# Latent stage: the last 64 latent columns on both halves of the partitions, and two short products of a round on row tiles side by side

## The chip, the cores and the metric

The kernel runs on one core of one Trainium2 chip. What is compared is the device time of one execution, in microseconds (us). The core has TensorE (PE; its weight loads are shown as PEld), VectorE (DVE), ScalarE (ACT), GpSimd (POOL) and SyncE (SP), each with a queue of its own. Matmul results go to PSUM, which has eight banks of 128 partitions x 512 f32 numbers.

## The reference, cut to what matters

The whole is a decoder of twelve blocks on a (16, 128, 256) input; each block is followed by a residual addition and a layer norm. The block of this change is latent attention (`_L2_attn_ref`), on 16 sequences of 128 tokens:

```python
c_q = _rmsnorm(x @ w_q_down.T, q_norm_w)            # 192 latent columns
q = (c_q @ w_q_up.T).reshape(b, t, H, NOPE + ROPE)  # 16 heads, 128 + 64
q_nope, q_rope = (q[..., :NOPE], q[..., NOPE:])
kv = x @ w_kv_down.T                                # 64 latent + 64 rotary
q_rope = _apply_rope(q_rope, cos, sin)
kv_up = (_rmsnorm(c_kv, kv_norm_w) @ w_kv_up.T).reshape(b, t, H, NOPE + VD)
scores = einsum(q_full, k_full) * scale             # causal, softmax
out = einsum(attn, v).reshape(b, t, H * VD) @ w_o.T
```

The kernel doesn't expand keys and values: the part of the key's up-projection is multiplied into the query's weights once (step "a"), that of the values into the output weights (step "b"), and the heads work on the 64 latent columns of the keys directly. A query of a head is then 64 rotary and 64 latent columns, both made from the 192 latent columns of `c_q`.

## The kernel before

The stage is the class `Latent` (line 1951 on). `order()` (L1997) writes the order of the work out by hand, and every engine walks it in the same order with its own method: `tensor` (L2020), `scalar` (L2119), `vector` (L2184), `gpsimd` (L2262). Engines meet through semaphores; `room[b]` is the event after which bank `b` may be written again, and each engine's queue is strictly in order.

The tokens are taken in four groups `g` of 512 (four sequences), and in each group eight pairs of heads: 32 units `u`. A round `t` of the loop runs several steps for units at different depths: "sw" and "q" (e = 0 and 1, the two heads of the pair) for u = t, "s" (scores) for u = t - 1, "t" (transposes of the probabilities) and "o" for u = t - 2, "acc" for u = t - 3. The order within a round is sw, t(0), s(0), q(0), t(1), s(1), q(1), o, acc. In rounds with t modulo 8 from 2 to 7 of the first three groups, one shared step for the next group stands ahead of "sw": dn, tr0, tr1, tr2, r0, r1.

- Step "dn" makes the latent columns of a group, "tr0" and "tr1" turn the first 128 and the last 64 of them (L2060), and ScalarE keeps them as `CQ[gs]` with 512 tokens in a row: `CQ[:, 0, :]` holds latent columns 0 to 127, `CQ[0:64, 1, :]` columns 128 to 191 (L2161).
- Step "sw" (L2078) makes the rotary part with its pairs exchanged, for both heads at once, in bank 2: two products, over 128 and over 64 rows. VectorE multiplies it by the sines into `M2` (L2223).
- Steps "q" (L2078 too) make rotary and latent part of one head in bank 3, again over 128 and over 64 rows. ScalarE copies the latent half to `QA` (L2171), VectorE multiplies the rotary half by the cosines (L2230) and adds `M2` (L2232). With L2232 bank 3 is free again: `room[3]`.
- Step "s" fills bank 4 with the causal mask (L2084) and four products (L2087). VectorE takes the maximum (L2236) and scales it (L2237), ScalarE the exponentials (L2177), VectorE the reciprocal (L2241), and GpSimd multiplies (L2268). `room[4]` comes with the exponentials.
- Step "t" is L2095 with VectorE's copy L2246, "o" L2102, "acc" L2113 in banks 0 and 1.

An f32 product shows as two matmul instructions ("passes") in the profile, each with a weight load of its own; a transpose shows as one. The weights are loaded by `load` (L1965) on SP's queue, in two sets with a semaphore each, while the stage before still runs.

## Time and profile before

| | |
|---|---|
| time, median of 3 runs | 4290.99 us (4288.17 to 4293.5) |
| the profiled execution's own time | 4302.71 us |
| its span, first to last instruction | 4300.9 us |
| its mean granted TensorE clock | 0.924 of full speed |
| busy: PE, DVE, ACT, POOL | 3705.8, 3159.7, 1976.4, 968.1 us |
| costliest lines of this stage on the page | L2078 (lCQ, lq) 142.6 us; L2177 90.6 us; L2268 66.6 us |

A share of busy time is a mean over twelve different stages. The groups of lines count a matmul from its start to the end of its flow through the array, so that back to back matmuls overlap by some tenths of a microsecond; how fast they follow each other is read from the starts. "Idle before" is time in which the engine had nothing running ahead of that group, and the name behind it what ended the wait.

### The profile page before, as it was taken

Reading aid. Unit: us, or ns where it says so; the run is one execution under the profiler, and the core shown is the slowest. Engines: PE = TensorE matmul, PEld = TensorE weight load, DVE = VectorE, ACT = ScalarE, POOL = GpSimd, SP = SyncE. Lnnn points to the kernel's source line nnn. Section 1 sums busy time; section 2 is a strip of 40 time slices with the busy share of each in tenths; the row PEclk is TensorE's granted clock in tenths of the full one; section 3 lists DMA queues with packets and bytes.
Section 4 is the critical chain, followed back from the end, with each engine's and each line's share of the span. In section 5 each row is a group of like instructions: output and inputs, shape, how many; then the busy total and the mean of one; then the engine's idle time right before and its main releaser. Section 6 shows DMA issues by size and latency. Waiting matters only on the chain.

```text
span 4300.9 us, 69538 instructions
## 1 busy us (share of the span) xinstructions
PE 3705.8 (86%) x25052; PEld 2244.1 (52%) x25068; DVE 3159.7 (73%) x7102; ACT 1976.4 (46%) x4701; POOL 968.1 (23%) x1237
## 2 busy tenths in 40 slices
PE   7799999998851858798999989869999999997985
PEld 3466666665531436644555555645555555554543
DVE  7788989887567665533566568758888888886678
ACT  4466666665521324212333334336556555563345
POOL 2433321344111000000111122023323233233220
PEclk9999999999975988898999989989999999997887
DMA  2222222222110100020000000300000000001000
GB/s 68 69 63 70 62 60 59 63 67 49 35 62 0 33 22 2 1 72 21 1 1 1 1 30 2 122 0 1 1 1 1 1 1 1 1 1 47 1 1 20
DMA packets 220707, 120.09 MB, mean 28 GB/s; under 512 B 115280, under 2 KB 213200, under 8 KB 219152
## 3 DMA queue, kind: packets, MB, share of 16 engines
q1 hardware_dynamic: 220368, 115.65, 9.6%
q8 instruction: 203, 3.33, 0.3%
q14 instruction: 136, 1.11, 0.1%
HBM read 100.89 MB, written 14.68 MB: 27 GB/s over the span
## 4 chain that ended last, share of the span: by engine, by line
PE 61%; DVE 24%; issue 5%; ACT 5%; POOL 3%; SPq 1%; DMA 1%; DVEq 0%; ACTq 0%; POOLq 0%
PE ps L305 20%; PE ps L3111 5%; PE ps L2078 3%; PE ps L2803 3%; PE ps L3099 3%; PE ps L2816 2%; PE ps L2782 2%; PE ps L497 2%; PE ps L2113 1%; POOL dTB L826 1%; PE ps L2596 1%; PE ps L575 1%; DVE macc L3243 1%; POOL dtmp L825 1%; DVE hMX L2871 1%
## 5 line engine op out<-in xcount | busy, mean ns | idle before, releaser
L305 PE MATMUL ps<-xT,min 128*128 128x512 f32 (+1 forms) x1072 | 536.8, 629 | 7.1 <-DVE mZ L3238 4.8
L3243 DVE SCALAR_TENSOR_TENSOR macc<-ps,mcw,macc 128x508 f32<-128x508 f32 (+2 forms) x408 | 302.9, 742 | 149.0 <-ACT macc L3167 139.4
L3181 ACT ACTIVATE mE<-ps,mcol 128x128 f32<-128x128 f32 x1024 | 291.3, 370 | 8.4 <-PE ps L3081 1.5
L305 PEld LDWEIGHTS ps<-xT,min 128*128 128x128 f32 (+1 forms) x1072 | 183.3, 191 | 191.2 <-issue 182.0
L3329 POOL TENSOR_TENSOR mE<-mE,mCB 128x512 f32<-128x512 f32 x128 | 163.7, 1279 | 482.3 <-ACT mE L3181 482.3
L3111 PE MATMUL ps<-mwo,macc 128*128 128x256 f32 x1024 | 246.1, 383 | 19.2 <-DVE macc L3277 19.2
L2841 ACT ACTIVATE hE<-ps 128x512 f32<-128x512 f32 x256 | 139.0, 594 | 223.4 <-PE ps L2803 223.4
L3336 POOL TENSOR_TENSOR mSQ<-mSQ,mtn 128x512 f32<-128x512 f32 x128 | 163.5, 1277 | 259.5 <-ACT mtn L3185 259.5
L2177 ACT ACTIVATE lP<-ps,lm 128x128 f32<-128x128 f32 x256 | 90.6, 366 | 266.1 <-DVE lm L2237 266.1
L3111 PEld LDWEIGHTS ps<-mwo,macc 128*128 128x128 f32 x1024 | 186.1, 191 | 47.3 <-DVE macc L3277 25.7
L2871 DVE TENSOR_REDUCE hMX<-ps 128x2 f32<-128x512 f32 x256 | 158.9, 684 | 57.9 <-PE ps L2782 57.9
L2268 POOL TENSOR_TENSOR lP<-lP,lm 128x512 f32<-128x512 f32 x64 | 66.6, 1041 | 574.5 <-DVE lm L2241 574.5
L821 POOL TENSOR_TENSOR dTB<-did,dNB 128x1024 f32<-128x1024 f32 (+1 forms) x10 | 28.7, 2871 | 664.4 <-DMA dNB<-d_N 599.0
L727 DVE SCALAR_TENSOR_TENSOR dav<-ps,dsmall,dav 128x508 f32<-128x508 f32 (+2 forms) x192 | 142.4, 742 | 47.2 <-ACT dav L598 42.5
L826 POOL TENSOR_TENSOR dTB<-dTB,dtmp 128x30 f32<-128x30 f32 (+11 forms) x300 | 170.3, 568 | 23.5
L727 DVE SCALAR_TENSOR_TENSOR daq<-ps,dsmall,daq 128x508 f32<-128x508 f32 (+2 forms) x192 | 142.5, 742 | 44.3 <-ACT daq L598 38.9
L2803 PE MATMUL ps<-hXE,hKE 32*128 32x256 f32 x1024 | 163.2, 440 | 13.4 <-DVE hXE L2877 7.9
L825 POOL TENSOR_TENSOR dtmp<-dNB,dTB 128x30 f32<-128x30 f32 (+11 forms) x300 | 155.4, 518 | 23.5
L497 PE MATMUL ps<-dKQ 128*128 128x256 f32 x512 | 137.7, 396 | 26.7 <-ACT dO L673 17.3
L727 DVE SCALAR_TENSOR_TENSOR dak<-ps,dsmall,dak 128x508 f32<-128x508 f32 (+2 forms) x192 | 142.3, 741 | 24.1 <-ACT dak L598 19.5
L3167 ACT ACTIVATE macc<-ps,ms,mcw 128x512 f32<-128x512 f32 x136 | 105.9, 779 | 116.6 <-PE ps L305 116.6
L2078 PE MATMUL ps<-lCQ,lq 128*128 128x512 f32 (+1 forms) x256 | 142.6, 656 | 17.7 <-DVE lQA L2232 17.7
(593 smaller groups left out, 8931.7 us busy)
## 6 DMA issues: line engine op xcount, KB each, us to landing
dwk<-in_L_attn_Wk SPq DMA_DIRECT2D x64, 128.0 KB, 2.3
dwq<-in_L_attn_Wq SPq DMA_DIRECT2D x64, 128.0 KB, 2.4
dwv<-in_L_attn_Wv SPq DMA_DIRECT2D x64, 128.0 KB, 2.4
dwg<-in_L_attn_Wg SPq DMA_DIRECT2D x64, 128.0 KB, 2.4
dwo<-in_L_attn_Wo SPq DMA_DIRECT2D x64, 128.0 KB, 2.6
min<-in_m_in SPq DMA_DIRECT2D x2, 4096.0 KB, 17.7
d_N<-dNT SPq DMA_DIRECT2D x256, 16.0 KB, 1.5
dTT<-d_TT SPq DMA_DIRECT2D x256, 16.0 KB, 1.9
```

The lines of the kernel that those rows point to most:

```text
L305: t = pe.matmul(out, w[:, j, :], self.c.xT[:, j, blk(g, 512)], start=j == 0, stop=j == 1)
L497: t = pe.matmul(bank(4 + i)[:, blk(j, 256)], self.KQ[s][:, 2 * i + j, 0, :], self.KQ[s][:, 2 * i + j, :, :], start=True, stop=True)
L727: x = dve.scalar_tensor_tensor(out=acc[:, :, 3 - j:T], in0=p[:, :, 0:T - 3 + j], scalar=small[:, 4 * k + j:4 * k + j + 1], in1=acc[:, :, 3 ...
L825: then(pool.tensor_tensor(part, bc(NB[:, s, s + 1:32], s, True), bc(TB[:, s, 0:s], 31 - s), ALU.mult))
L826: then(pool.tensor_tensor(low, low, part, ALU.subtract))
L2078: t = pe.matmul(bank(b), w, self.CQ[gs][0:K, i, :], start=i == 0, stop=i == 1)
L2803: t = pe.matmul(bank(4 + i)[:, blk(lt, 256)], self.KE[x][r, e, blk(lt)], self.XE[x][r, e, :], start=True, stop=True)
L2871: m = dve.tensor_reduce(self.MX[y][:, k, 32 * r:32 * r + 32:16], bank(r).rearrange("p (e n) -> p e n", e=2), AX.X, ALU.max, negate=True)
L3111: t = pe.matmul(bank(j // 2)[:, blk(j % 2, 256)], self.acc[s][:, blk(j)], self.wo[:, i, :], start=i == 0 and j % 2 == 0, stop=i == 31 and ...
L3181: x = act.activation(self.E[s][:, e, blk(j)], bank(4 + e)[:, blk(j)], ACT.Exp, bias=self.col[:, 4 * g + j, 0, 2 * i + e:2 * i + e + 1])
L3243: x = dve.scalar_tensor_tensor(out=acc[:, :, 3 - j:T], in0=p[:, :, 0:T - 3 + j], scalar=self.cw[:, i, j:j + 1], in1=acc[:, :, 3 - j:T], op ...
L3329: pool.tensor_tensor(g4(self.E[s][:, 0, :]), g4(self.E[s][:, 0, :]), self.CB[g % 2][:, :, :], ALU.mult).then_inc(*self.m0.up)
```

## The change

The last 64 latent columns are kept on both halves of the partitions (`CQ[:, 1, :]`, 128 partitions). To get them there, "tr1" adds to each of its four transposes a product with the identity into partitions 64 to 127 of bank 6, and ScalarE's copy takes all 128 partitions, with a scale laid out likewise (`n2`). The query weights of these 64 rows lie on both halves too for the rotary part (one more load of 512 KB; two small ones for `n2`); for the latent part, made in step "a", heads alternate: the even head of a pair lies on partitions 64 to 127, the odd one on 0 to 63. In "a" the outputs of the second kind go to the two column halves in turn, and ScalarE copies them with two instructions instead of one.

In the rounds, the product of q(e=0) over 64 rows moves ahead into "sw": between the product over 128 rows into bank 2 and that over rows 0 to 63 into bank 2 stands the one over rows 64 to 127 into bank 3. It opens the sum in bank 3, and q(e=0) closes it with its product over 128 rows, without a wait on bank 3. Instead "sw" waits for `room[3]`. Step q(e=1) stays as it was.

```diff
@@ -1961,15 +1962,16 @@
         self.q, self.sw_ = c.f32("lq", 2, 16, 128), c.f32("lsw", 2, 1024)
         self.qT, self.kvT = c.f32("lqT", 16, 192), c.f32("lkvT", 16, 2, 64)
         self.wo, self.cs = c.f32("lwo", 16, D), c.f32("lcs", 2, T)
+        self.n2 = c.f32("ln2", 3)
 
     def load(self, sp):
         i = self.ins
         self.may_load(sp)
         self.fetch(sp, 0, (self.dn[:, :, :], i["l_dn"].rearrange("(c p) n -> p c n", p=128)), (self.nw[:, :], i["l_nw"]),
-                   (self.cs[:, :, :], i["c_rope"]))
+                   (self.n2[64:128, :], i["l_nw"][0:64, :]), (self.n2[0:64, :], i["l_nw"][0:64, :]), (self.cs[:, :, :], i["c_rope"]))
         q = self.q[:, :, :, :].rearrange("p c h n -> p c (h n)")
         self.fetch(sp, 1, (self.qT[:, :, :], i["l_qT"]), (self.kvT[:, :, :, :], i["l_kvT"]),
-                   (q[:, 0, :], i["l_q"][0:128, :]), (q[0:64, 1, :], i["l_q"][128:192, :]),
+                   (q[:, 0, :], i["l_q"][0:128, :]), (q[0:64, 1, :], i["l_q"][128:192, :]), (q[64:128, 1, :], i["l_q"][128:192, :]),
                    (self.sw_[:, 0, :], i["l_sw"][0:128, :]), (self.sw_[0:64, 1, :], i["l_sw"][128:192, :]),
                    (self.wo[:, :, :], i["l_wo"].rearrange("(h p) n -> p h n", p=128)))
 
@@ -2019,7 +2021,7 @@
 
     def tensor(self, pe):
         c, bank, room = self.c, self.c.bank, self.c.room
-        pe.wait_ge(self.dma[1], 112)
+        pe.wait_ge(self.dma[1], 128)
         for step, g, u, e in self.order():
             s, gs, pr = u % 4, g % 2, u % 8
             if step == "a":
@@ -2027,8 +2029,8 @@
                 rows = 64 if i else 128
                 pe.wait_ge(*room[g])
                 for h in range(8):
-                    t = pe.matmul(bank(g)[0:rows, blk(h, 64)], self.qT[:, 8 * n + h, 128 * i:128 * i + rows], self.kvT[:, 8 * n + h, 0, :],
-                                  start=True, stop=True)
+                    to = bank(g)[blk(1 - h % 2, 64), blk(h, 64)] if i else bank(g)[:, blk(h, 64)]
+                    t = pe.matmul(to, self.qT[:, 8 * n + h, 128 * i:128 * i + rows], self.kvT[:, 8 * n + h, 0, :], start=True, stop=True)
                 t.then_inc(*self.am.up)
                 room[g] = self.ac.at(g + 1)
             elif step == "b":
@@ -2044,7 +2046,7 @@
             elif step == "dn":
                 pe.wait_ge(*c.xt_ready(self.n, g))
                 if g == 0:
-                    pe.wait_ge(self.dma[0], 48)
+                    pe.wait_ge(self.dma[0], 80)
                 for h in range(2):
                     pe.wait_ge(*room[6 + h])
                     for j in range(2):
@@ -2058,6 +2060,8 @@
                 pe.wait_ge(*self.cn.at(g + 1))
                 for j in range(4):
                     t = pe.transpose(bank(6)[0:n, blk(j)], self.CN[gs][:, j, lo:lo + n], c.ident[:, :])
+                    if n == 64:
+                        t = pe.matmul(bank(6)[64:128, blk(j)], self.CN[gs][:, j, lo:lo + n], c.ident[:, :], start=True, stop=True)
                 t.then_inc(*self.trn.up)
                 room[6] = self.kept.at(3 * g + i + 1)
             elif step in ("r0", "r1"):
@@ -2067,15 +2071,24 @@
                 room[7] = self.rot.at(2 * g + n + 1)
             elif step in ("sw", "q"):
                 n, b = (0, 2) if step == "sw" else (e + 1, 3)
-                pe.wait_ge(*room[b])
+                if (n, e) != (1, 0):
+                    pe.wait_ge(*room[b])
                 if n == 0:
                     pe.wait_ge(*self.kept.at(3 * g + 3))
                     pe.wait_ge(*self.kr.at(g + 1))
                 if u == 0:
                     pe.wait_ge(*self.ac.at(4))
-                for i, K in enumerate((128, 64)):
-                    w = self.sw_[0:K, i, blk(pr)] if n == 0 else self.q[0:K, i, 2 * pr + e, :]
-                    t = pe.matmul(bank(b), w, self.CQ[gs][0:K, i, :], start=i == 0, stop=i == 1)
+                CQ = self.CQ[gs]
+                if n == 0:
+                    pe.wait_ge(*room[3])
+                    pe.matmul(bank(2), self.sw_[:, 0, blk(pr)], CQ[:, 0, :], start=True, stop=False, skip_group_check=True)
+                    pe.matmul(bank(3), self.q[64:128, 1, 2 * pr, :], CQ[64:128, 1, :], start=True, stop=False, skip_group_check=True)
+                    t = pe.matmul(bank(2), self.sw_[0:64, 1, blk(pr)], CQ[0:64, 1, :], start=False, stop=True, skip_group_check=True)
+                elif e == 0:
+                    t = pe.matmul(bank(3), self.q[:, 0, 2 * pr, :], CQ[:, 0, :], start=False, stop=True, skip_group_check=True)
+                else:
+                    pe.matmul(bank(3), self.q[:, 0, 2 * pr + 1, :], CQ[:, 0, :], start=True, stop=False)
+                    t = pe.matmul(bank(3), self.q[0:64, 1, 2 * pr + 1, :], CQ[0:64, 1, :], start=False, stop=True)
                 t.then_inc(*self.up.up)
                 room[b] = self.m2.at(u + 1) if n == 0 else self.qa.at(2 * u + e + 1)
             elif step == "s":
@@ -2119,8 +2132,8 @@
     def scalar(self, act, own):
         c, bank = self.c, self.c.bank
         self.before(act)
-        act.wait_ge(self.dma[0], 48)
-        act.wait_ge(self.dma[1], 112)
+        act.wait_ge(self.dma[0], 80)
+        act.wait_ge(self.dma[1], 128)
         for step, g, u, e in self.order():
             s, gs = u % 4, g % 2
             if step == "last":
@@ -2128,10 +2141,15 @@
                 continue
             if step == "a":
                 n, i = divmod(g, 2)
-                rows = 64 if i else 128
                 act.wait_ge(*self.am.at(g + 1))
-                act.copy(self.q[0:rows, i, 8 * n:8 * n + 8, :].rearrange("p (q e) n -> p q (e n)", e=2)[:, :, 64:192],
-                         bank(g)[0:rows, :].rearrange("p (q n) -> p q n", n=128)).then_inc(*self.ac.up)
+                if i == 0:
+                    x = act.copy(self.q[:, 0, blk(n, 8), :].rearrange("p (q e) n -> p q (e n)", e=2)[:, :, 64:192],
+                                 bank(g).rearrange("p (q n) -> p q n", n=128))
+                else:
+                    for e in range(2):
+                        half = blk(1 - e, 64)
+                        x = act.copy(self.q[half, 1, 8 * n + e:8 * n + 8:2, half], bank(g)[half, :].rearrange("p (q e n) -> p q e n", e=2, n=64)[:, :, e, :])
+                x.then_inc(*self.ac.up)
             elif step == "b":
                 act.wait_ge(*self.bm.at(g + 1))
                 act.activation(self.B[:, blk(g, 2), :], bank(2 + g).rearrange("p (q n) -> p q n", q=2), ACT.Copy,
@@ -2151,14 +2169,13 @@
                 o.then_inc(*self.sqs.up)
             elif step in ("tr0", "tr1", "tr2"):
                 i = int(step[2])
-                n = self.TURNS[i][1]
                 act.wait_ge(*self.trn.at(3 * g + i + 1))
                 if g >= 2 and i == 0:
                     act.wait_ge(*self.up.at(24 * g - 24))
                 if g >= 2 and i == 2:
                     act.wait_ge(*self.sc.at(16 * g - 16))
                 if i < 2:
-                    x = act.activation(self.CQ[gs][0:n, i, :], bank(6)[0:n, :], ACT.Copy, scale=self.nw[0:n, i:i + 1])
+                    x = act.activation(self.CQ[gs][:, i, :], bank(6), ACT.Copy, scale=self.n2[:, 1:2] if i else self.nw[:, 0:1])
                 else:
                     act.activation(self.KK[gs][64:128, 0, :], bank(6)[64:128, :], ACT.Copy, scale=self.nw[64:128, 2:3])
                     x = act.activation(self.KK[gs][0:64, 1, :], bank(6)[0:64, :], ACT.Copy, scale=self.nw[0:64, 2:3])
@@ -2184,7 +2201,7 @@
     def vector(self, dve, own):
         c, bank = self.c, self.c.bank
         dve.wait_ge(*self.c.xn.at(4 * self.n))
-        dve.wait_ge(self.dma[0], 48)
+        dve.wait_ge(self.dma[0], 80)
 
         def then(ins):
```

## Rows read from the trace of the kernel before

**Rows 1.** TensorE in a stretch of the stage: length, busy us (and instructions) per engine, granted clock.
```profile
2060.00:2160.00 100.00, 93.22 (x456) 53.61 (x455) 54.50 (x117) 34.39 (x145) 13.54 (x13) 1.00 0.00 1
```

**Rows 2.** Chain of waits of one round: start us, us, what ran.
```profile
2406.32 0.07 DVE lm L2241
2406.43 0.69 DVE lQA L2230
2407.15 1.02 DVE lQA L2232
2408.22 2.18 PE ps L2078 x4
```

**Rows 3.** The stage's waits (2000 to 2490): us in total, times, longest.
```profile
PE ps L2078 <- DVE lQA L2232: 17.7, 29, 1.5
PEld ps L2084 <- ACT lP L2177: 15.9, 32, 2.3
```

**Rows 4.** TensorE's timeline of the same round: start us, us, count at the end.
```profile
2400.05 2.07 PE L2078 MATMUL ps<-lCQ,lsw 128*128 128x512 f32 x4
2403.65 2.08 PE L2078 MATMUL ps<-lCQ,lq 128*128 128x512 f32 x4
2405.66 0.66 PE L2095 MATMUL ps<-ident,lP 128*128 128x128 f32 x4
2406.35 0.39 PE L2084 MATMUL ps<-identb,neg 128*128 128x512 bf16 x1
2410.32 1.09 PE L2102 MATMUL ps<-lPT,lCN 128*64 128x128 f32 x16
```

**Rows 5.** Timeline: four passes without a change of tiling.
```profile
2330.95 1.88 PE L305 MATMUL ps<-xT,ldn 128*128 128x512 f32 x4
```

**Rows 6.** Timeline: passes on four, and on two row tiles, in other stages.
```profile
1514.34 2.00 PE L1289 MATMUL ps<-rQE,rKT 32*128 32x512 f32 x16
2533.38 1.13 PE L2803 MATMUL ps<-hXE,hKE 32*128 32x256 f32 x8
```

**Rows 7.** Timeline: the end of that round and the next "sw".
```profile
2412.08 0.91 DVE L2232 TENSOR_TENSOR lQA<-lQA,lM 64x512 f32<-64x512 f32 x1
2412.97 0.41 PEld L2078 LDWEIGHTS ps<-lCQ,lsw 128*128 128x128 f32 x2
2413.18 0.59 PE L2078 MATMUL ps<-lCQ,lsw 128*128 128x512 f32 x1
```

**Rows 8.** Timeline: four transposes in a round, and tr1 in the prologue.
```profile
2198.69 0.60 PE L2060 MATMUL ps<-ident,lCN 128*128 128x128 f32 x4
2199.13 0.59 PE L2078 MATMUL ps<-lCQ,lsw 128*128 128x512 f32 x1
1993.75 1.06 PE L2060 MATMUL ps<-ident,lCN 128*64 128x128 f32 x4 [0.78 <-ACT lCQ L2161]
```

**Rows 9.** Timeline: rounds 0 and 1.
```profile
2014.90 4.08 PE L2078 MATMUL ps<-lCQ,lsw 128*128 128x512 f32 x4
2015.73 0.69 DVE L2232 TENSOR_TENSOR lQA<-lQA,lM 64x512 f32<-64x512 f32 x1
2021.02 3.34 PE L2078 MATMUL ps<-lCQ,lq 128*128 128x512 f32 x4
```

**Rows 10.** Timeline: ScalarE after the copies of step "a".
```profile
1983.11 0.33 ACT L2147 ACTIVATE lCN<-ps 128x192 f32<-128x192 f32 x1 [1.34 <-PE ps L311]
```

**Rows 11.** The clock: stretches with it at half or kept, and one q(e=1).
```profile
2160.17:2170.41 10.24, 9.21 (x32) 5.60 (x33) 4.76 (x9) 4.23 (x17) 2.08 (x2) 0.50 0.00 0
2470.78:2474.20 3.42, 3.42 (x22) 2.77 (x22) 1.03 (x3) 1.71 (x9) 0.44 (x1) 0.50 0.02 5
1508.00:1521.00 13.00, 6.01 (x72) 2.98 (x64) 12.28 (x40) 6.67 (x17) 0.00 (x0) 1.00 0.00 0
1547.00:1560.00 13.00, 7.07 (x77) 3.99 (x70) 10.52 (x35) 3.27 (x9) 0.00 (x0) 0.76 0.00 0
2163.31 3.92 PE L2078 MATMUL ps<-lCQ,lq 128*128 128x512 f32 x4
```

## The prediction

> **What bounds the kernel now.** I read the stage first by stretches, then one round as a chain of waits, then the waits, then TensorE's own timeline. Only the Latent stage changes (2006 to 2480 us, some 11% of the span); in it TensorE is busy 93 us of a stretch of 100 [rows 1], which looks like a TensorE bound. The chain of waits of one round says something narrower [rows 2]. A round is 13.13 us here: "sw" starts at 2400.05 and again at 2413.18 [rows 4, 7]. TensorE works without a gap from q(e=1) at 2408.22 [rows 2] over "o", "acc", "sw", "t" and "s" to the start of q(e=0) at 2403.65 in the round: 4.96 us up to the next sw, and 3.60 us from sw to q(e=0). The remaining 4.57 us, from 2403.65 to 2408.22, are not TensorE's: the chain leaves it for the maximum, four exponentials on ScalarE, the reciprocal, and the two VectorE instructions on the query, L2230 (0.69) and L2232 (1.02). Only then is bank 3 free and q(e=1) may start. The list of waits agrees: TensorE waits for L2232 29 times in the stage, 17.7 us in all, and its weight load of the second "s" waits for the exponentials 32 times, 15.9 us [rows 3]. So of TensorE's work, what stands between q(e=0) and q(e=1) is covered, and everything else in the round is path.
>
> **The change, part by part.**
>
> *The short product taken out of q(e=0).* A 128x512 f32 product is two passes. Without a change of tiling, four passes take 1.88 us [rows 5]; with a last one of 0.59 that is (1.88 - 0.59)/3 = 0.43 a pass. The four of q(e=0) take 2.08, 0.20 more for going from 128 to 64 rows [rows 4]. After the change q(e=0) is two passes, over at 2403.65 + 0.86 = 2404.51, where the transposes of "t" came at 2405.66: 1.15 us of TensorE time per round are gone. But they are gone under cover. The second "s" needs bank 4, freed by exponentials that end at about 2406.3 and don't depend on q(e=0); its first instruction stays at 2406.35 [rows 4]. L2230 comes behind the reciprocal in VectorE's queue, at 2406.43 [rows 2], while its data were there when TensorE went on to "t" at 2405.66 [rows 4]; earlier data don't move it. So q(e=1) stays at 2408.22. TensorE idles about 1.4 us before the second "s" instead of 0.2 to 0.3, and still 0.59 us before q(e=1). Gain in a regular round: 0.
>
> *The pair in "sw".* "sw" was two passes over 128 rows and two over 64. Now two passes over 64 other rows (64 to 127, into bank 3) stand between them. Do they run beside the old ones? The trace has row tiles of f32: sixteen passes of 512 columns on four row tiles take 2.00 us, and eight passes of 256 columns on two row tiles of 32 rows 1.13 [rows 6]. One after the other, sixteen passes would take 16 x 0.43 = 6.9; four slots of 0.43 and a tail of 0.2 to 0.3 are 2.0. So tiles in different banks run side by side, both passes of a product with both of its neighbour. The bounds are 0 us per round and, if they ran in turn, +0.86 us. I take 0: same number type, same width of 512, banks differing as there.
>
> *The new wait.* "sw" now waits until the previous round's L2232 for e=1 has let go of bank 3. Behind the waiting instruction stands all of TensorE: "t" and "s", and behind these the chain. In rounds without a shared step L2232 runs 2412.08 to 2412.99, and the weight load of "sw" started at 2412.97, its matmul at 2413.18 [rows 7]. A wait is passed on in some 0.05 us (L2232 ends at 2408.17, TensorE starts at 2408.22 [rows 2]), so the load moves to 2413.04 and needs about 0.1 before the matmul can stream (q(e=1), started from idle, took 2.18 against 2.08 [rows 2, 4]): 2413.15, just in time. Twelve rounds have this margin of 0.2 us; a shared step gives the others 0.4 us or more. Between 0 and 0.1 us each: I take 12 x 0.05 = +0.6. It hangs on a thread: each 0.1 us by which the chain of e=1 is later costs 1.2 us.
>
> *The first rounds.* There the chain is not full yet. In round 0 L2230 waits for the product itself, so 1.15 us fewer before it are a gain; but L2232 of e=1 ended at 2016.42, 1.5 us after the next "sw" had started at 2014.90, so the new wait takes it back. Round 1 runs at half clock and its q(e=0) took 3.34 us [rows 9]. Together -2 to +1; I take -1.
>
> *The doubled transpose, tr1.* Per group four 64-column transposes get four f32 matmuls, eight passes, on the other column half. The transposes alone cost 0.44 us in a round (from 2198.69 to 2199.13, where the next product starts) and 1.06 at half clock in the prologue [rows 8]. Column tiles of the same form do run side by side: "o" does sixteen passes of 128 columns in 1.09 us [rows 4], 0.11 for each two. With eight slots of 0.11 instead of four that is +0.44; in turn, +0.9. Three rounds and a prologue at half clock: 3 x 0.44 + 0.9 = +2.2 to twice as much. I take +2.5. ScalarE's copy goes from 64 to 128 partitions, at the same 0.68 us.
>
> *Step "a", the loads.* Of the 64 passes of "a", 32 now alternate between column halves and may overlap (-0.9 at most); ScalarE copies in two pieces instead of one, some 0.3 us more, before 1.34 us of idle time [rows 10]. I take 0. One load of 512 KB and two tiny ones are added on SP's queue; they go out with the stage's other weights while the stage before still runs, and nothing waits for them alone. I take 0 here too.
>
> *The clock.* This is the part that has a price. Apart from the first rounds, the granted clock fell to half (1.2 of 2.4 GHz) in each of the three rounds with a "dn" step, where TensorE waits longest: 2160.17 to 2170.41 is the second [rows 11]. Its cost is in the rows: q(e=1) took 3.92 us there against 2.18 [rows 2, 11]. A dense stretch brings it back sooner: 2470.78 to 2474.20 was at half, 3.4 us long [rows 11], and costs half of that, 1.7. The change makes every regular round emptier between 2404.95 and 2408.22: out of 3.3 us TensorE works only in "s", 1.1. Whether such a pattern loses the clock the trace answers both ways: 1508 to 1521 kept 1.00 with TensorE busy 6.01 of 13 us, but 1547 to 1560, busy 7.07, had 0.76 [rows 11]. So 0 to 10 additional falls in the 27 rounds that are neither the first two nor hold a "dn", at 1.7 us each when q(e=1) starts in one: 0 to +17. I take three: +5.
>
> The Trainium skill ("TensorE: Matmul & The Clock Gate", section "HAM oscillation — how this bites in real kernels") says that repeated pauses of TensorE throw its clock back to half every time round a loop. Taken strictly here it would hit in most rounds, some 27 x 1.7 = +46 us by my rows; the stretch at 1508 speaks against so strict a reading, the one at 1547 for part of it.
>
> **The sum.** 0 (rounds) + 0 (pair) + 0.6 (wait) - 1 (first rounds) + 2.5 (tr1) + 5 (clock) = +7.1. The profiled execution took 4302.7 us (span 4300.9), so its like would take 4310; the median of the runs shown is 11.7 lower, 4291, and gives 4298.
>
> **The rivals.**
> *A, the passes pay.* If q(e=1) could start earlier by what q(e=0) lost, 29 rounds would give up to 1.15 us: -33, about 4260. For it: TensorE's 93%. Against it: the 0.59 us it already idles there, and VectorE's queue, in which L2230 is never the one waiting. The Trainium skill ("TensorEngine Tiling (Array Packing)", section "Theoretical Speedup") promises up to twice the speed for a dimension of at most 64. As a mechanism of this kernel that is six short passes in the time of four, 32 x 0.86 = 28 us and 4263, if they were path. Chance 0.06 for both.
> *B, the clock falls often*, eight to ten times or more: 4291 + 2 + 10 x 1.7 = 4310. Place: q(e=1), "o", "acc" at half clock. It decides from about four falls on. Chance 0.22.
> *C, the pair doesn't pair*: two more passes in turn in "sw", on the path: 32 x 0.86 = 27 and a few of B, 4320. The change would then not do what it says. Against: [rows 6]. Chance 0.05.
> *D, the wait at "sw" bites* by 0.5 us in twelve rounds: 4291 + 6 + 7 = 4304. Chance 0.07.
> *The forecast*, nothing won in the regular rounds and a few us lost: 4292 to 4303. Chance 0.60.
>
> A difference of 0.2%, 8.6 us, is about what this kernel's measurement tells from none. Faster than 4282.4 is nearly A alone: 0.08. Slower than 4299.6 is B, C, D and a third of the forecast: 0.44. Within: 0.48. The range takes in the forecast and most of B and D, 4284 to 4314.
>
> **What would show it.** TensorE's line L2078 before q(e=1) still waits for L2232, with as many waits and the same 0.59 us; the weight load of the second "s" waits about 1.2 us more per round, so near 50 us in all. The regular round without a shared step stays at 13.1 us; six passes of "sw" take 2.1 us with two starts a few ns apart. Stretches at half clock inside 2060 to 2460 rise from two starts to about five. Wrong if the round gets shorter than 13.0 (A), "sw" takes over 2.8 us (C), or the first pass of "sw" is seen waiting for L2232 by more than 0.1 us (D).

## The result, and the profile after

The changed kernel takes 4306.3 us (median of six runs, 4302.6 to 4311.6); the kernel before, measured beside it, 4290.9 (six runs, 4282.1 to 4293.5). The ratio is 1.004, with a 95% interval of 1.0027 to 1.0053: 15.4 us, or 0.4%, slower. The forecast was 4298. It had the sign of the sum and the mechanism of the regular round, and it was 8 us too low: the change costs twice what was worked out.

The page of the changed kernel begins so: the span, then busy time of each engine with its share and its instructions.

```profile
span 4309.8 us, 69637 instructions
PE 3681.2 (85%) x25084; PEld 2240.8 (52%) x25100; DVE 3162.6 (73%) x7102; ACT 1979.1 (46%) x4703; POOL 966.4 (22%) x1237
```

TensorE was busy 3705.8 us before and is busy 3681.2 now, so the change saves the engine 25 us of busy time and the kernel is slower. To see how, compare the same round of the Latent stage as in [rows 2, 4, 7]. TensorE's timeline of the kernel after (start us, us, engine, line, operation, what is written and read, count, and in brackets the idle time before with its releaser):

```profile
2401.71 1.05 PE L2084 MATMUL ps<-lCQ,lsw 128*128 128x512 f32 x2
2402.69 0.69 PE L2085 MATMUL ps<-lCQ,lq 64*128 64x512 f32 x1
2402.69 0.69 PE L2086 MATMUL ps<-lCQ,lsw 64*128 64x512 f32 x1
2403.22 0.59 PE L2085 MATMUL ps<-lCQ,lq 64*128 64x512 f32 x1
2403.23 0.59 PE L2086 MATMUL ps<-lCQ,lsw 64*128 64x512 f32 x1
2403.75 0.66 PE L2108 MATMUL ps<-ident,lP 128*128 128x128 f32 x4
...
2405.34 1.02 PE L2088 MATMUL ps<-lCQ,lq 128*128 128x512 f32 x2
2406.21 0.60 PE L2108 MATMUL ps<-ident,lP 128*128 128x128 f32 x4
2408.04 0.39 PE L2097 MATMUL ps<-identb,neg 128*128 128x512 bf16 x1 [1.23 <-ACT lP L2194]
2408.26 1.05 PE L2100 MATMUL ps<-lKK,lQA 128*128 128x128 f32 x8
2409.91 1.12 PE L2090 MATMUL ps<-lCQ,lq 128*128 128x512 f32 x2 [0.59 <-DVE lQA L2249]
2410.97 1.12 PE L2091 MATMUL ps<-lCQ,lq 64*128 64x512 f32 x2
2412.02 1.09 PE L2115 MATMUL ps<-lPT,lCN 128*64 128x128 f32 x16
2413.04 1.99 PE L2126 MATMUL ps<-lB,lM 128*128 128x256 f32 x8
2414.87 0.62 PE L2084 MATMUL ps<-lCQ,lsw 128*128 128x512 f32 x1
```

The reader is to see four things. First, the two short products (L2085 of the query, L2086 of "sw") start within 0.01 us of each other, twice: the pair runs side by side, and six passes take 2.04 us (2401.71 to the transposes of "t" at 2403.75), where four took 2.0 before (2400.05 to 2402.05). Second, q(e=0) (L2088) is down to two passes. Third, the time so won has become an idle gap of 1.23 us (0.2 to 0.3 before) ahead of the second "s", which waits for ScalarE's exponentials. Fourth, q(e=1) (L2090) comes 8.20 us after the start of "sw", as before (8.17), after the same 0.59 us of waiting for VectorE's second instruction on the query. The round is 13.16 us (2401.71 to 2414.87); it was 13.13 [rows 4, 7].

The waits of the stage say the same for all rounds (engine, line, what it waited for: us in all, times, longest). Against [rows 3], the wait at q(e=1) is 18.1 us for 17.7, with the same 29 times, and the weight load's wait at the second "s" is 49.6 us for 15.9:

```profile
PEld ps L2097 <- ACT lP L2194: 49.6, 32, 2.5
PE ps L2097 <- ACT lP L2194: 41.2, 32, 2.1
PE ps L2090 <- DVE lQA L2249: 18.1, 29, 1.5
```

So the regular round is a draw, and the loss lies elsewhere. There are two places. The first is tr1. Before, it was four transposes of 64 columns and made its round 0.44 us longer (13.57 us for 13.13), as four of 128 columns do in [rows 8]. Now (timeline of the kernel after):

```profile
2065.89 0.27 PE L2062 MATMUL ps<-ident,lCN 128*64 128x128 f32 x1
2066.10 0.43 PE L2064 MATMUL ps<-ident,lCN 128*64 128x128 f32 x2
2066.46 0.30 PE L2062 MATMUL ps<-ident,lCN 128*64 128x128 f32 x1
2066.69 0.43 PE L2064 MATMUL ps<-ident,lCN 128*64 128x128 f32 x2
...
2068.24 0.70 PE L2084 MATMUL ps<-lCQ,lsw 128*128 128x512 f32 x1
```

L2062 is a transpose, L2064 the plain product on the other column half. They don't overlap: a product (two passes) starts 0.21 us after its transpose, the next transpose 0.36 us after that. A pair of one of each takes 0.57 to 0.60 us (2065.89 to 2066.46 to 2067.05), and four pairs 2.35 us instead of 0.44. In the prologue, at half clock, tr1 takes 3.96 us instead of 1.06 [rows 8].

The second place is the clock. Stretches of the kernel after, with the columns of [rows 1, 11] (length, busy us and instructions of TensorE, its weight loads, VectorE, ScalarE and GpSimd, granted clock, DMA):

```profile
2076.83:2083.65 6.82, 6.82 (x24) 3.29 (x23) 2.57 (x6) 2.67 (x10) 1.04 (x1) 0.50 0.00 0
2244.08:2250.91 6.83, 6.83 (x24) 3.31 (x23) 2.57 (x6) 2.67 (x10) 1.04 (x1) 0.50 0.00 0
2380.61:2387.44 6.83, 6.83 (x23) 3.32 (x23) 2.64 (x6) 2.67 (x10) 1.04 (x1) 0.50 0.00 0
2060.00:2140.00 80.00, 70.29 (x361) 41.06 (x360) 40.90 (x75) 27.39 (x108) 11.36 (x12) 0.96 0.00 1
2300.00:2480.00 180.00, 156.28 (x830) 92.98 (x829) 107.44 (x229) 62.01 (x251) 27.07 (x26) 0.98 0.00 1
```

The first three are new: half clock (1.2 of 2.4 GHz) in rounds without a "dn" step, 6.8 us long each. With the two in "dn" rounds there are five starts between 2060 and 2460, where the kernel before had two. (A start of such a stretch is called a fall from here on.) What one costs can be read off TensorE's timeline of the second:

```profile
2243.77 1.80 PE L2090 MATMUL ps<-lCQ,lq 128*128 128x512 f32 x2 [0.59 <-DVE lQA L2249]
2245.50 2.07 PE L2091 MATMUL ps<-lCQ,lq 64*128 64x512 f32 x2
2247.50 1.97 PE L2115 MATMUL ps<-lPT,lCN 128*64 128x128 f32 x16
2249.40 2.72 PE L2126 MATMUL ps<-lB,lM 128*128 128x256 f32 x8
2251.96 1.02 PE L2084 MATMUL ps<-lCQ,lsw 128*128 128x512 f32 x2
```

Start to start, and against the regular round above: q(e=1) 3.73 us for 2.11, "o" 1.90 for 1.02, "acc" 2.56 for 1.83. Together 8.19 for 4.96, so 3.2 us for each fall; the three rounds are 16.4 to 16.9 us long.

The account of the stage, from the first pass of step "a" to the last of "acc", is 524.3 us after and 507.7 before: +16.5 in these two executions, beside +15.4 between the medians. That the two agree is in part luck: the whole executions (4311.6 and 4302.7 us) differ by 8.9 only, since outside the stage, where TensorE's work is the same, the one of the kernel after was 7.7 us shorter. Its parts: +3.9 in the prologue (from the first pass of "a" to the first "sw", 35.1 us for 31.2); +5.9 in the three rounds with a tr1 (15.5 to 15.7 us for 13.6); +9.8 in the three rounds with a new fall (3.3 + 3.2 + 3.3); -3.0 in two "dn" rounds, whose own half-clock stretches fell more kindly; -0.8 in round 1; and the rest, +0.8, in all others, a regular round being 13.16 for 13.13 us. The 0.9 us that pairing saves in step "a" (64 passes in 5.16 us, 6.08 before) is inside the prologue's sum, and so is the stretch at half clock there, which is 17.1 us long for 10.2 before.

### The profile page after: what moved, and what is told of

The parts are those of the page before. It is cut to its first block and busy times, and to the rows that moved or that the text cites. A ratio compares the mean times of both kernels' runs of the same rounds, so it can differ in the third digit from the quotient of the medians.

```text
span 4309.8 us, 69637 instructions
## 1 busy us (share of the span) xinstructions
PE 3681.2 (85%) x25084; PEld 2240.8 (52%) x25100; DVE 3162.6 (73%) x7102; ACT 1979.1 (46%) x4703; POOL 966.4 (22%) x1237
## 5 line engine op out<-in xcount | busy, mean ns | idle before, releaser
L3189 ACT ACTIVATE mtn<-macc 128x512 f32<-128x512 f32 x136 | 85.9, 632 | 154.9 <-DVE macc L3260 154.9
```

## The experiments

The kernel before was timed beside each group of experiments: its median was 4289.0 us beside e1 to e4, 4290.0 beside e5 to e8, and 4288.0 beside e9 to e11. Each experiment has one trace, and where the clock falls differs from execution to execution; so a number of falls stands for that trace alone.

### Is the time won in q(e=0) worth anything?

*e1_hole*, an edit of the kernel before:

```
-                for i, K in enumerate((128, 64)):
+                parts = (128,) if (n, e) == (1, 0) else (128, 64)
+                for i, K in enumerate(parts):
...
-                    t = pe.matmul(bank(b), w, self.CQ[gs][0:K, i, :], start=i == 0, stop=i == 1)
+                    t = pe.matmul(bank(b), w, self.CQ[gs][0:K, i, :], start=i == 0, stop=i == len(parts) - 1)
```

> The kernel before, with the product over the last 64 latent columns left out of q(e=0) and nothing put in its place (so the even heads' queries lack it). Theory (cover and clock): q(e=1) still waits for VectorE's L2232, so the regular round stays at 13.13 us and nothing is won; TensorE idles about 1.4 us before the second s, and the granted clock falls in more rounds than the three with a dn step: 0 to 5 more falls of about 3.3 us each, total 0 to +15 us against before, with no part of it from tr1 or from the new wait. Rival (the passes pay): 29 rounds shorter by up to 1.15 us, -33 us. Rival (the whole cost is in the rest of the change: tr1, the wait): same time as before within 2 us and no more falls than before.

Measured: 4291.8 us (4285.3 to 4300.7, ten runs), ratio 1.001 [1.0, 1.0019]. TensorE's timeline of one of its rounds:

```profile
2398.86 2.07 PE L2079 MATMUL ps<-lCQ,lsw 128*128 128x512 f32 x4
2402.46 1.02 PE L2079 MATMUL ps<-lCQ,lq 128*128 128x512 f32 x2
2405.15 0.39 PE L2085 MATMUL ps<-identb,neg 128*128 128x512 bf16 x1 [1.23 <-ACT lP L2178]
2407.03 2.18 PE L2079 MATMUL ps<-lCQ,lq 128*128 128x512 f32 x4 [0.59 <-DVE lQA L2233]
2411.99 0.59 PE L2079 MATMUL ps<-lCQ,lsw 128*128 128x512 f32 x1
```

Two passes per round, 64 in all, are gone and nothing replaces them, yet the round is still 13.13 us (2398.86 to 2411.99), with the same gaps of 1.23 and 0.59 us as in the changed kernel. Rival A is dead: in this order of work the short product in q(e=0) is free in a regular round. And three half-clock stretches stand outside the "dn" rounds of this trace too (from 2320.4, 2364.7 and 2446.7), none before: in this order of work the hole alone brings them. Only where the chain is not yet full is anything won: round 0 takes 7.37 us for 8.60, and round 1, at full clock here, 12.99 for 16.61.

### What of the loss is tr1, and what the clock?

*e2_tr1_pair*, the kernel after with tr1 as plain products on both column halves:

```
-                    t = pe.transpose(bank(6)[0:n, blk(j)], self.CN[gs][:, j, lo:lo + n], c.ident[:, :])
-                    if n == 64:
-                        t = pe.matmul(bank(6)[64:128, blk(j)], self.CN[gs][:, j, lo:lo + n], c.ident[:, :], start=True, stop=True)
+                    if n == 128:
+                        t = pe.transpose(bank(6)[:, blk(j)], self.CN[gs][:, j, lo:lo + n], c.ident[:, :])
+                    else:
+                        for x in range(2):
+                            t = pe.matmul(bank(6)[blk(x, 64), blk(j)], self.CN[gs][:, j, lo:lo + n], c.ident[:, :], start=True, stop=True)
```

> The changed kernel with tr1 made of plain products alone, two column halves for each block, and no transposes between them. Theory: in the changed kernel each switch between a transpose and a product drains the array, 8 times a tr1, so a tr1 round is 15.48 us; with one kind only the column halves pair and the round is about 14.1 us (13.57 before, + 4 slots of 0.11 and a start of 0.1). 3 rounds x 1.4 and about 2.5 in the prologue: -6 to -7 us against the changed kernel, 4300. Rival: the drain belongs to the change of column half, not of kind; then the round stays at 15.5 us and the time at 4306.

*e3_fill*, the kernel after with a product that nothing needs (two passes of 512 columns into the free bank 2) where TensorE idles before the second "s":

```
                 b = 4
+                if e == 1:
+                    pe.wait_ge(*room[2])
+                    pe.matmul(bank(2), self.q[:, 0, 0, :], self.q[:, 0, 0:4, :].rearrange("p h n -> p (h n)"), start=True, stop=True)
```

> The changed kernel with two more passes of 128x512 f32 (0.86 us) on idle bank 2, between t(e=1) and the second s, where TensorE waits 1.4 us; their result is not used. Theory (clock): the three falls outside the dn rounds (6.8 us long, 3.3 us lost each) go away and nothing else moves: -8 to -10 us against the changed kernel, about 4297, with more work done. Rival (work is work): the filler delays the second s or the clock falls anyway: same or up to +25 us.

*e4_fill_pair*, both edits:

> Both: the filler and tr1 of plain products. Theory: -15 to -17 against the changed kernel, so the time of the kernel before, 4289 to 4293: the whole loss is then accounted for by tr1 and the clock. Rival: the new wait at sw has a share of its own that these two don't reach: 4296 or more.

Measured, with the ratio to the kernel before beside them:

| kernel | median us | runs | ratio | against the change's 1.004 |
|---|---|---|---|---|
| e2_tr1_pair | 4290.4 (4280.7 to 4302.1) | 11 | 1.0001 [0.9991, 1.0011] | -17 us |
| e3_fill | 4295.0 (4289.2 to 4300.8) | 11 | 1.0013 [1.0005, 1.0022] | -12 us |
| e4_fill_pair | 4282.5 (4275.5 to 4298.1) | 12 | 0.9985 [0.9975, 0.9994] | -24 us |

In e2_tr1_pair's timeline tr1 is sixteen passes of one kind, in 1.02 us (2056.13 to 2057.15) instead of 2.35:

```profile
2056.13 1.09 PE L2066 MATMUL ps<-ident,lCN 128*64 128x128 f32 x16
2057.15 1.12 PE L2086 MATMUL ps<-lCQ,lsw 128*128 128x512 f32 x2
```

Its tr1 rounds last 14.3 us (15.5 to 15.7 with the alternation, 13.6 before) and its prologue 31.0 us (35.1, and 31.2 before). The prologue's gain is more than the shorter tr1: the half-clock stretch in it is 10.2 us long in the two kernels with paired products and 17.1 in the two with the alternation. These terms add up to 4.1 + 3 x 1.3 = 8 us. Rounds 0 to 2 are another 4.0 us shorter, mostly round 1 (13.50 us for 15.77), in which e2's trace keeps the full clock; and e2's trace has four falls outside the "dn" rounds, one more than the kernel after, which takes 3.2 back. In all the stage is 9 us shorter between these two traces. The measured difference is 17, with an uncertainty of some 7 from the two intervals, and 6 to 7 had been expected. What it has over the 9 of the stage stays open; the two traced executions differ by 7 us more outside the stage.

In e3_fill the same round reads, on TensorE (the filler is L2098), and its stretches below it:

```profile
2432.05 0.60 PE L2111 MATMUL ps<-ident,lP 128*128 128x128 f32 x4
2432.49 1.02 PE L2098 MATMUL ps<-lq 128*128 128x512 f32 x2
2433.89 0.39 PE L2100 MATMUL ps<-identb,neg 128*128 128x512 bf16 x1 [0.37 <-ACT lP L2197]
...
2435.76 1.12 PE L2090 MATMUL ps<-lCQ,lq 128*128 128x512 f32 x2 [0.59 <-DVE lQA L2252]
```

```profile
2060.00:2140.00 80.00, 74.33 (x381) 42.83 (x379) 41.93 (x77) 26.85 (x107) 11.44 (x11) 1.00 0.00 1
2300.00:2480.00 180.00, 165.60 (x895) 98.39 (x895) 106.17 (x225) 62.22 (x257) 28.08 (x27) 1.00 0.00 1
```

The filler changes no moment of the round (13.16 us, the second "s" when the exponentials end), and the clock keeps 1.00 in the stretches where the kernel after had 0.96 and 0.98. In both kernels with the filler no fall stands outside the first and the "dn" rounds; in the four with this round, the hole and no filler (the kernel after, e1, e2, e9) there are three, three, four and six. The interval of e3 (1.0005 to 1.0022) lies clear of the change's (1.0027 to 1.0053). The cost of the emptier round is its clock, and it can be bought back with useless work. The Trainium skill ("TensorE: Matmul & The Clock Gate", section "A second HAM failure mode: psum-queue depth-cycling") describes such a kernel, in which short pauses between groups of matmuls bring the clock down again and again; here the gaps are 1.23 and 0.59 us, and the trace agrees in kind, in 3 of 27 rounds.

With both repaired the change comes out 6 us ahead of the kernel before (ratio 0.9985), better than the draw that was expected; its stage is 6.5 us shorter in the traces. Half of that is round 1, which takes 13.50 us in e4_fill_pair's trace, at full clock, for 16.61, as in e2_tr1_pair's and, near it, in e1_hole's.

### Does grouping the two kinds help?

*e9_tr1_group*, the kernel after with four transposes first and the four products behind them:

```
                 for j in range(4):
                     t = pe.transpose(bank(6)[0:n, blk(j)], self.CN[gs][:, j, lo:lo + n], c.ident[:, :])
-                    if n == 64:
-                        t = pe.matmul(bank(6)[64:128, blk(j)], self.CN[gs][:, j, lo:lo + n], c.ident[:, :], start=True, stop=True)
+                if n == 64:
+                    for j in range(4):
+                        t = pe.matmul(bank(6)[64:128, blk(j)], self.CN[gs][:, j, lo:lo + n], c.ident[:, :], start=True, stop=True)
```

> The changed kernel with tr1's four transposes first and its four products behind them: the same work, but 2 switches of kind (one into the products, one out of tr1 to sw) where the changed kernel has 8. Theory (each switch drains the array, about 0.2 us): tr1 takes 0.44 + 0.2 + 8 x 0.11 = 1.5 us from its first transpose to sw instead of 2.35, and the round after which it stands is 14.7 us where the changed kernel has 15.48. Rival (the products themselves are slow, not the switches): 15.4 us.

Its timeline:

```profile
2051.20 0.60 PE L2062 MATMUL ps<-ident,lCN 128*64 128x128 f32 x4
2051.73 1.09 PE L2065 MATMUL ps<-ident,lCN 128*64 128x128 f32 x8
2052.75 0.70 PE L2085 MATMUL ps<-lCQ,lsw 128*128 128x512 f32 x1
```

tr1 takes 1.55 us and the round 14.7 to 14.8, as expected. The work is the same as in the kernel after, four transposes and four products; only the order differs, and 0.8 us are gone. So the alternation is a cost of its own. It can be sized: the twelve passes (one for a transpose, two for a product) at 0.11 us, one after the other, are 1.32 us. That leaves 1.03 us of the 2.35 for eight changes of kind (the last is the one into "sw") and 0.23 of the 1.55 for two, so 0.12 to 0.13 us each. It isn't the change of column half: e2_tr1_pair changes it at every product, and its sixteen passes take 1.02 us. Of the 1.9 us that tr1 grew by in a round, then, 0.9 are passes in turn and 1.0 changes of kind. The one run of the kernel took 4309.6 us, with six falls outside the "dn" rounds; as a time of the kernel it says nothing.

### Does the new wait cost anything?

*e10_wait_before*, the kernel before with the change's wait and nothing else:

```
                 if n == 0:
+                    pe.wait_ge(*room[3])
                     pe.wait_ge(*self.kept.at(3 * g + 3))
```

> The kernel before, with sw waiting for bank 3 (L2232 of e=1 of the round before) as in the change, and nothing else. Theory: it costs 0.03 us in the 12 rounds without a shared step (13.16 for 13.13), and 1.5 us or less at the start: 0 to +2 us, the same as before. Rival (the wait is a cost of the change worth naming): a weight load that can't run ahead costs 0.1 us or more in each such round, and the time is 5 us or more above before.

Measured: 4286.0 us (4279.7 to 4292.0, ten runs), ratio 0.9996 [0.9986, 1.0006]. The regular round is 13.13 us, so the wait costs nothing there. Round 0 grows from 8.60 to 10.42 us. The stage as a whole stays (507.2 us for 507.7), but only because the half-clock stretch of round 2 is 6.8 us long in this trace and 10.2 in that of the kernel before, which makes the round 2.0 us shorter. So the wait costs about 2 us in the first round and none behind it, and the time, with an interval of -6 to +3 us, can't tell that from nothing.

### When would the change pay?

If the free time of q(e=0) is covered by VectorE's and ScalarE's chain, a kernel with a shorter chain should uncover it. VectorE takes the reciprocal, which waits for the last exponential, before the two instructions on the query. *e5_dve_before* turns this round in the kernel before: a new step "rcp" behind q, and TensorE itself waits for ScalarE's part of the query (shown in part; a wait for it stands before the products of "s" too).

```
-            for step, u, e in (("sw", a, 0), ("t", c, 0), ("s", b, 0), ("q", a, 0), ("t", c, 1), ("s", b, 1), ("q", a, 1), ("o", c, 0),
+            for step, u, e in (("sw", a, 0), ("t", c, 0), ("s", b, 0), ("q", a, 0), ("rcp", b, 0), ("t", c, 1), ("s", b, 1), ("q", a, 1), ("rcp", b, 1), ("o", c, 0),
...
+                if n and 2 * u + e:
+                    pe.wait_ge(*self.lat.at(2 * u + e))
...
-                dve.wait_ge(*self.lat.at(2 * u + e + 1))
...
+            elif step == "rcp":
+                me = self.m[s][:, e, :]
```

> The kernel before with another order on VectorE alone: L2230 and L2232 of a head now stand ahead of the reciprocal that waits for the exponentials, and TensorE waits for ScalarE's copy itself instead of L2232 doing so. The change under study is not in it. Theory (VectorE's queue is what covered the short product): without the change q(e=0) ends 2.2 us after the second half starts, so q(e=1) can start at about 3.95 instead of 4.57 us: 0.6 us a round, 27 rounds, -16 us, 4273. Rival (the exponentials and ScalarE's copy bound it too): same time as before.

*e6_dve_after* is the same edit on the kernel after with the paired tr1; the wait for q(e=0)'s bank stands in "sw", where its first product now is:

> The changed kernel with tr1 of plain products and the same new order on VectorE. Theory: q(e=0) ends 1.15 us sooner, L2230 and L2232 run while ScalarE does the exponentials, and q(e=1) starts right behind the second s, at 3.8 us: 0.8 us a round against 4.57 and 0.2 more than the same order gives without the change. -21 us against e2, 4268. TensorE still idles 1.4 us before the second s, so falls of the clock stay. Rival (the change is worth nothing in any order): no faster than e5 plus what e2 and before differ by, 4274 or more.

*e7_acc_before* and *e8_acc_after* take these two and move "acc" from the end of the round to right behind q(e=0), into the place the chain covers (shown against the kernel before, which has no "rcp"):

```
-            for step, u, e in (("sw", a, 0), ("t", c, 0), ("s", b, 0), ("q", a, 0), ("rcp", b, 0), ("t", c, 1), ("s", b, 1), ("q", a, 1), ("rcp", b, 1), ("o", c, 0),
-                               ("acc", d, 0), ("close", d, 0), ("stats", t - 4, 0), ("rsqrt", t - 5, 0), ("scale", t - 6, 0)):
+            for step, u, e in (("sw", a, 0), ("t", c, 0), ("s", b, 0), ("q", a, 0), ("acc", d, 0), ("rcp", b, 0), ("t", c, 1), ("s", b, 1), ("q", a, 1), ("rcp", b, 1), ("o", c, 0),
+                               ("close", d, 0), ("stats", t - 4, 0), ("rsqrt", t - 5, 0), ("scale", t - 6, 0)):
```

> e5 with step acc (1.72 us of TensorE, its data long there) moved from the end of the round to right behind q(e=0), where TensorE would wait. Theory: TensorE is then the bound, and without the change its round is 3.60 + 2.0 + 1.7 + 0.4 + 1.1 + 2.1 + 1.1 = 12.0 us, 1.1 less than 13.13: -30 us, 4260, with fewer falls of the clock. Rival: a later second s lengthens the chain by as much as the end of the round gets shorter: as e5.

> e6 with step acc moved likewise. Theory: now the passes that the change saves are path: the round is 3.60 + 0.86 + 1.7 + 0.4 + 1.1 + 2.1 + 1.1 = 10.9 us by TensorE, but sw has to wait for L2232 of e=1, which ends about 8.0 us after sw's q(e=0) started: 11.6 us. 0.4 to 1.1 us a round less than e7: 4235 to 4250. Rival (the change pays nowhere): the same as e7 within 5 us.

*e11_acc_split* parts the "acc" of e8: three of its four column blocks there, the last behind "o".

> e8 with step acc parted: three of its four products behind q(e=0), the last one behind o as before. Theory (in e8 sw waits for L2232 of e=1, which follows q(e=1) by 3.5 us, while TensorE has half a microsecond to spare at the end of the round): the second s then starts right as the exponentials end, q(e=1) 0.33 us sooner, and the round is 11.15 us for 11.49: -9 us against e8, 4217. Rival (ScalarE's exponentials already bound e8, so that q(e=1) can't come sooner): the same as e8.

| kernel | median us | runs | ratio | regular round us |
|---|---|---|---|---|
| e5_dve_before | 4269.6 (4261.5 to 4270.6) | 5 | 0.9945 [0.9932, 0.9959] | 12.28 |
| e6_dve_after | 4265.0 (4259.7 to 4266.0) | 5 | 0.9937 [0.9924, 0.995] | 12.28 |
| e7_acc_before | 4254.4 (4248.2 to 4263.7) | 6 | 0.9918 [0.9903, 0.9933] | 12.12 |
| e8_acc_after | 4226.3 (4221.5 to 4232.1) | 5 | 0.9855 [0.984, 0.9869] | 11.49 |
| e11_acc_split | 4227.4 (4224.4 to 4235.1) | 5 | 0.9863 [0.9844, 0.9882] | 11.17 |

One round of e8_acc_after, TensorE and the instructions of VectorE that matter:

```profile
2352.31 1.10 PE L2088 MATMUL ps<-lCQ,lsw 128*128 128x512 f32 x2 [0.58 <-DVE lQA L2253]
...
2355.99 1.02 PE L2092 MATMUL ps<-lCQ,lq 128*128 128x512 f32 x2
...
2356.86 1.89 PE L2131 MATMUL ps<-lB,lM 128*128 128x256 f32 x8
...
2357.06 0.68 DVE L2252 TENSOR_TENSOR lQA<-ps,lcs 64x512 f32<-64x512 f32 x1
...
2357.77 0.68 DVE L2253 TENSOR_TENSOR lQA<-lQA,lM 64x512 f32<-64x512 f32 x1
2358.58 0.60 PE L2113 MATMUL ps<-ident,lP 128*128 128x128 f32 x4
2358.66 0.18 DVE L2264 RECIPROCAL lm<-lm 128x4 f32<-128x4 f32 x1 [0.21 <-ACT lP L2199]
...
2360.13 1.02 PE L2094 MATMUL ps<-lCQ,lq 128*128 128x512 f32 x2
...
2363.80 0.67 PE L2088 MATMUL ps<-lCQ,lsw 128*128 128x512 f32 x1 [0.57 <-DVE lQA L2253]
```

What follows, in order. e5: the order on VectorE alone gives 0.85 us a round; bank 3 is free before q(e=1) is due, and its wait is gone. e6: the change adds nothing to the regular round even here, since q(e=1) is issued behind the second "s", and that waits for the exponentials (1.23 us in its trace too); my reason for its gain was wrong. Its 4.6 us over e5 are within the two intervals, and in the traces rounds 1 and 2 are 6.7 us shorter. The other half of its expectation failed too: the falls were to stay, and its trace has none outside the "dn" rounds. So in this trace the gap of 1.23 us does not bring them by itself; what this kernel no longer has is the 0.59 us ahead of q(e=1). e7 and e8: with "acc" behind q(e=0), TensorE has work until the exponentials are done, and the second "s" runs without a wait in the round shown. Now TensorE is the bound between q(e=0) and q(e=1), and what the change takes out there is path: 12.12 us becomes 11.49, and the kernel is 28 us faster with the change (its tr1 as products) than without (4226.3 and 4254.4), more than the 10 to 25 us that was expected. From the first to the last "sw" the traces have 386.8 us for 411.2, so 24 of the 28. In the regular rounds the new wait bites here for the first time: "sw" stands 0.57 us for L2253 of e=1. e11 moves TensorE's work away from that wait and gets its round of 11.17 us, but not its time: from the first to the last "sw" it is 388.8 us for 386.8. The traces have the sum: eleven of the twelve regular rounds are 0.32 us shorter, 3.5 in all; the rounds with a shared step are no shorter (12.70 us for 12.59), the three with tr1 1.2 us longer in all, and the three "dn" rounds 3.6, with half-clock stretches of 10.2, 3.4 and 10.2 us for 3.4, 10.2 and 3.4. The last is where the clock happened to fall, so one trace does not say what e11 is worth; why the rounds with a shared step gain nothing stays open.

e8_acc_after is the best version: 1.45% or some 62 us below the kernel before, and 80 us below the changed one by medians.

## Why the prediction was right and where it failed

The range held, 4284 to 4314, but the case called the forecast, 4292 to 4303 with a chance of 0.60, did not: 4306.3 lies above it, where only rivals were expected. The chances also don't add up as written: B, C, D and a third of the forecast for a time above 4299.6 are 0.22 + 0.05 + 0.07 + 0.20 = 0.54, not 0.44.

*The short product out of q(e=0): 0.* Right, with the numbers named: the same count and 18.1 us of waiting at q(e=1), 49.6 us at the second "s" where "near 50" was forecast. e1_hole shows the cover by itself, e5 to e8 what it consists of: VectorE's order, which alone held q(e=1) by 0.85 us, and under it the exponentials.

*The pair in "sw": 0.* Right. Both passes of a product run beside both of its neighbour, and six passes take the time of four, 2.04 us. Rival C is out.

*The new wait: +0.6.* At most that: e10_wait_before puts it at 0 in the regular round (interval -6 to +3 us for the kernel), and the regular round of the kernel after is 0.03 us longer. It was near its threshold, as the step said; e8 shows it at 0.57 us once the rest of the round is shorter.

*The first rounds: -1.* -0.8 in round 1 and +0.1 in round 0 by the traces, and the working holds: the hole alone makes round 0 1.2 us shorter (7.37 for 8.60, e1_hole), the wait alone 1.8 longer (10.42, e10_wait_before), and the change has both (8.67). How long rounds 1 and 2 are depends on where the clock falls.

*Step "a": 0.* Mis-sized by a little: the alternation between column halves was let go as "-0.9 at most", and 0.9 is what it saved.

*tr1: +2.5.* This step failed. "Column tiles of the same form do run side by side: 'o' does sixteen passes of 128 columns in 1.09 us" is true of products among products: e2_tr1_pair, in which they pair, takes 1.02 us. But the change puts a transpose and a product in turn, and these are not of the same form. They don't pair, which is 0.9 us, and each change from one kind to the other costs 0.12 to 0.13 us more, eight times, which is 1.0: four pairs take 2.35 us in place of 0.44. So +1.9 to 2.1 a round, not +0.44, and +2.9 in the prologue, not +0.9; with the longer stretch at half clock that the prologue then has, and less the 0.9 of step "a", the term is +9.8 by the traces of before and after (3.9 + 5.9). That the longer tr1 is what lengthens that stretch is not shown; both traces with the alternation have it, no other. The rows could have warned: "in turn" was my upper bound, and even it, 0.9, was too low, as it priced a change of kind at nothing. The nearest row was that of a change from 128 to 64 rows, 0.20 us [rows 4, 5], and I had used it further up; at eight times 0.2 it would have been too dear, but it names the right cost.

*The clock: +5.* The number of falls was right, three, and their place too, but the number was luck: it was picked from 0 to 10 without a working, and the like kernels had three to six. The price was wrong. The 1.7 us came from [rows 11], by a stretch of 3.4 us at the dense end of the stage and by q(e=1) alone at half clock, without the "o" and "acc" behind it. The new falls last 6.8 us, and nearly all of it is path: 3.2 us each, 9.8 in all. Two "dn" rounds gave 3.0 back by chance of place. That these falls come from the hole was an argument then; e3_fill and e4_fill_pair show it, since 0.86 us of useless work in the hole removes them and 12 and 8 us of time (e3 against the change, e4 against e2). The strict reading of the Trainium skill ("TensorE: Matmul & The Clock Gate", section "HAM oscillation — how this bites in real kernels") that I set beside it, a fall in most rounds and +46, is not what the traces have: three to six in 27.

*The sum.* +16.5 in the stage by the traces, +15.4 by the medians, where +7.1 was worked out. Of the 9.4 us between, tr1 is +7.3 (with "a" in it), the price of a fall +4.8, the "dn" rounds -3.0, and the small terms +0.3. Rival B gave nearly this time, 4310, but with ten falls at 1.7; there were three at 3.2 and a tr1 that cost four times what it was put at. The likeliest case had the right mechanism for the round and the wrong size for both of its costs.

## What to carry to other kernels

Ask of each instruction taken away what waits at the end of the cover it stood in: with TensorE 93% busy, 64 passes fewer gave nothing in the regular rounds until a step from the path ("acc") was moved into the place they left. Then the same change was worth 28 us. Work removed under a cover can have a price of its own, the clock: an engine that idles more often may lose it in the work behind the gap, and the price of a fall is half its length as far as that is path, read from a stretch in the same kind of round.

When an instruction is added between others, compare its kind with its neighbours' before its length: transposes and products one by one took 2.35 us, in two groups 1.55, all as products in pairs 1.02.

## What the runs showed of the hardware

- A 64-column f32 transpose and a plain f32 product on the other column half do not overlap; in turn they cost 0.59 us a pair at full clock and about 1.0 at half (3.96 us for four pairs). Of the 2.35 us for four pairs, 1.32 are the twelve passes one after the other and 1.03 the eight changes of kind, an estimate of 0.13 us each; the same work in two groups took 1.55 us.
- Two f32 products on row tiles of 64 into different banks start together and finish together, both passes: six passes of 512 columns in the time of four.
- Gaps of 1.23 and 0.59 us in a round of 13.13 to 13.16 went with half clock in three to six of 27 rounds, for 6.8 us each time (four traces); gaps of 0.37 and 0.59 in none (two traces), and a gap of 1.23 alone, in a round of 12.28, in none (one trace, e6_dve_after).
- In the prologue the half clock lasted 17.1 us in the two traces with the alternating tr1, 10.2 in ten others and 6.8 in e9_tr1_group. What decides it is not shown.
